# Attention in turns of two steps, with the array's small tiles kept together

## The reference

```python
x = x + 0.5 * ffn(layernorm(x))          # 256 -> 1024 -> 1024 -> 256
x = x + attention(layernorm(x))          # 16 heads of 16 dims
x = x + 0.5 * ffn(layernorm(x))          # the same weights as the first

# ffn: each weight matrix is +1 or -1, from a boolean
h = s0 * (concat([x, -x]) @ w0); h = relu(h) * 2
h = s1 * (h @ w1);               h = relu(h) * 2
h = s2 * (h @ w2)

# attention, per batch and head
scores = softmax(q @ k.T / sqrt(16))     # 2048 x 2048 per head and batch
att = scores @ v
out = att @ wo.T + bo
```

## Time and profile before

| what | value |
|---|---|
| median of 3 runs | 1521.37 us |
| the profiled execution: time, span | 1521.35 us, 1517.2 us |
| PE busy | 1509.4 us (99%), 12471 matmuls |
| ACT busy | 1129.3 us (74%) |
| DVE busy | 573.5 us (38%) |
| POOL busy | 59.6 us (4%) |
| granted TensorE clock | 1.00 of full speed |

### The profile page before, as it was taken

One profiled execution on the slowest core, in us unless ns is written; L12 is line 12 of the kernel. 1 busy time (PEld: TensorE's weight loads), 2 busy tenths in 40 slices (PEclk: granted clock), 3 DMA queues, 4 the chain that ended last, 5 costly groups with the idle time before them and its releaser, 6 DMA issues.

```text
span 1517.2 us, 31574 instructions
## 1 busy us (share of the span) xinstructions
PE 1509.4 (99%) x12471; PEld 604.4 (40%) x12471; DVE 573.5 (38%) x1298; ACT 1129.3 (74%) x1654; POOL 59.6 (4%) x65
## 2 busy tenths in 40 slices
PE   8999999999999999999999999999999999999999
PEld 4555455334333333433333333333333333333354
DVE  7645764511431253234333233241332323332462
ACT  3221222898898998899889889888888988998721
POOL 2010011001000100010100000000000000000000
PEclk9999999999999999999999999999999999999999
DMA  4122323212231331232223113112213212311110
GB/s 139 42 84 48 78 77 113 75 44 81 83 82 41 96 96 41 67 105 71 81 54 95 40 53 95 40 40 67 81 40 68 81 40 54 107 47 34 36 42 16
DMA packets 110139, 101.46 MB, mean 67 GB/s; under 512 B 55846, under 2 KB 95526, under 8 KB 109990
## 3 DMA queue, kind: packets, MB, share of 16 engines
q1 hardware_dynamic: 109158, 98.60, 22.8%
q10 hardware_dynamic: 832, 0.79, 0.2%
HBM read 61.87 MB, written 25.43 MB: 58 GB/s over the span
## 4 chain that ended last, share of the span: by engine, by line
PE 99%; DVE 0%; DMA 0%; ACT 0%; issue 0%
PE psum L890 31%; PE psum L852 30%; PE psum L874 16%; PE psum L752 12%; PE psum L764 3%; PE psum L740 3%; PE psum L771 2%; PE psum L784 1%; PE psum L777 0%; DMA x_sb<-in_x 0%; DVE stats L1032 0%; DVE xn L974 0%; PE psum L712 0%; DVE x_sb L989 0%; ACT xn L913 0%
## 5 line engine op out<-in xcount | busy, mean ns | idle before, releaser
L944 ACT ACTIVATE prob<-psum 128x512 f32<-128x512 f32 (+1 forms) x1438 | 1016.6, 784 | 120.0 <-PE psum L874 115.5
L890 PE MATMUL psum<-prob,v_sb 128*17 128x512 f32 x4096 | 489.4, 595 | 0.0
L874 PE MATMUL psum<-q_st,k_st 64*128 64x512 f16 x2048 | 350.1, 379 | 0.2
L917 ACT ACTIVATE h_hi<-psum 128x512 f16<-128x512 f32 x183 | 109.6, 604 | 211.9 <-PE psum L752 160.7
L982 DVE TENSOR_SCALAR h_hi<-psum 128x512 f16<-128x512 f32 x73 | 50.5, 692 | 434.0 <-PE psum L852 434.0
L984 DVE SCALAR_TENSOR_TENSOR h_lo<-psum,h_hi 128x512 f16<-128x512 f32 x256 | 168.7, 687 | 83.4 <-ACT h_hi L917 80.9
L890 PEld LDWEIGHTS psum<-prob,v_sb 128*17 128x17 f32 x4096 | 95.2, 96 | 263.0 <-issue 166.4
L874 PEld LDWEIGHTS psum<-q_st,k_st 64*128 64x128 f16 x2048 | 82.5, 94 | 279.1 <-ACT prob L944 210.7
L852 PE MATMUL psum<-h_hi,w 64*128 64x512 f16 x1184 | 152.1, 376 | 0.2 <-ACT h_hi L917 0.2
L852 PE MATMUL psum<-h_lo,w 64*128 64x512 f16 x1184 | 152.0, 376 | 0.0
L752 PE MATMUL psum<-h_hi,w 128*128 128x512 f16 x432 | 102.1, 379 | 0.0
(11 more groups left out here) (109 smaller groups left out, 857.1 us busy)
## 6 DMA issues: line engine op xcount, KB each, us to landing
k_st<-k_halves SPq DMA_DIRECT2D x64, 512.0 KB, 4.4
q_halves<-piece SPq DMA_DIRECT2D x32, 256.0 KB, 2.5
q_st<-q_halves SPq DMA_DIRECT2D x64, 128.0 KB, 5.0
x_rows<-x_sb SPq DMA_DIRECT2D x16, 256.0 KB, 2.2
k_halves<-piece SPq DMA_DIRECT2D x16, 256.0 KB, 2.8
att_rows<-o_sb SPq DMA_DIRECT2D x128, 32.0 KB
x_sb<-x_rows SPq DMA_DIRECT2D x8, 512.0 KB, 4.1
att_t<-att_rows SPq DMA_DIRECT2D x16, 256.0 KB
```

Source lines behind the costliest of these rows:

```text
L874: mm = pe.matmul(psum[:, score_bank[h + r], :], k_st[rows, slot, t * P:(t + 1) * P], q_st[rows, slot, :], start=True, stop=True)
L890: mm = pe.matmul(psum[32 * j:32 * j + va, O_BANK, :], v_sb[:, b * key_tiles + t, GROUP * g4 + j, :], prob[:, h % PROBS, :], start=(t == 0) ...
L917: act.activation(hi, psum[:, bank, :], ACT.Relu).then_inc(act_done, 1)
L944: act.activation(prob[:, to:to + count, :], psum[:, bank:bank + count, :], ACT.Exp, scale=score_scale / QK_SCALE ** 2).then_inc(exp_sem, 1)
```

## The change

Attention now goes in turns of two steps, after a first step that has scores and side slots alone. A turn begins with wide work: four times a group of side slots (`GAP`: 4 of l2, 8 of l3, 1 of qk, 2 of v or `out`) and a score pair behind each. Then come four tiles of products, with a narrow score pair behind each. In turns of l1 the second half of the 16 slots stands in the narrow part and is narrow too.

A product with v is split into two matmuls, one for each half of 64 keys; the lower half goes into bank 4 and the upper into bank 5 (`O_BANKS`), and `dve_o` copies one and adds the other. Narrow scores and narrow slots have each 128-column matmul cut into four of 32 columns (`columns_of`), so everything in the narrow part runs on tiles of 64 rows and 32 columns. The score ring has four banks, always used as two neighbouring pairs, and all exps take two banks. `sq` moves from the score ring to the side banks, between products.

PE's program, steady work of l2, before: the end of one step and the start of the next (L874 scores, L890 products with v).

The diff, cut:

```diff
+    narrow: bool = False
     mate: object = None
...
-    SCORES = [0, 1, 2, 3, 4]
-    O_BANK = 5
+    O_ZEROED = 1
+    SCORES = [0, 1, 2, 3]
+    O_BANKS = [4, 5]
...
         if behind == blocks:
             steps.append(Step("range", blocks - 1))
         if ahead is not None:
             steps += [Step("l1", ahead, m) for m in range(2)]
-            if after and not early:
-                steps.append(Step("sq", behind))
             steps += [Step("l1", ahead, m) for m in range(2, kh)]
...
     ahead_of_attention = [s.kind in FILLS for s in side[:[(s.kind, s.u) for s in side].index(("l2", qblocks + 1))]]
-    in_turn = SCORES[:4] + SHARED + SCORES[4:]
+    in_turn = SCORES + SHARED + O_BANKS[1:]
...
-    PAIRS = {"l1": (4, 4), "l2": (5, 3), "l3": (10, 6), "qk": (1, 1), "v": (2, 2), "out": (2, 2)}
+    GAP = {"l1": 4, "l2": 4, "l3": 8, "qk": 1, "v": 2, "out": 2}
+    o_left = numbers.held[O_BANKS[1]]
...
                 find[bank.kind, bank.u, bank.m] = bank
             s.hi = 0
         lo, s.hi = s.hi, s.hi + slots
-        work.append(replace(s, lo=lo, hi=s.hi, n=2 * s.n, mate=t))
+        work.append(replace(s, lo=lo, hi=s.hi, n=2 * s.n, mate=t, narrow=narrow))
         if s.hi == 2 * s.n:
             s.lo, s.hi = 0, s.n
...
-
-    for n in range(att_steps):
-        work.append(Step("att", n))
-        lay_scores(n)
-        work.append(Step("score", n, 0))
+    scores_left = [numbers.held[bank] for bank in SCORES]
+
+    def lay_score(no, narrow=False):
+
+        n, pair = divmod(no, STEP_BANKS // 2)
+        if pair == 0:
+            work.append(Step("att", n))
+        work.append(Step("score", n, pair, narrow=narrow))
+
+    def lay_values(tile):
+        work.append(Step("values", tile // 2, tile % 2))
+
+    def lay_turn(n):
+
         lay_idle(n)
         if side[0].kind != "l2":
             lay_long(math.inf)
-        elif n >= 4 and side[0].hi + sum(PAIRS["l2"]) < 2 * FILLS["l2"][0]:
+        else:
             lay_long(1.0)
 
-        for between, slots in enumerate(((5, 3), (3, 3), (3, 2), (3, 2))[n] if n < 4 else PAIRS[side[0].kind]):
-            lay_pair(slots)
-            work.append(Step("score", n, 1 + between))
-        if n == 0:
-            lay_pair(8)
-        if columns and not side[0].n:
-
-            lay_exps(n, ((0, 1), (1, 2), (3, 1), (4, 1), (5, 2), (7, 1)))
-            lay_column(columns.pop(0))
+    def lay_column():
+
+        if side[0].kind in ("sq", "range"):
+            lay(side.pop(0), SHARED, False)
+
+    lay_score(0)
+    lay_score(1)
+    lay_turn(0)
+    lay_pair(5)
+    lay_score(2)
+    lay_pair(5)
+    lay_score(3)
+    lay_pair(6)
+
+    for n in range(1, att_steps, 2):
+        no, tile, whole = 4 * n, 2 * (n - 1), n + 1 < att_steps
+        lay_turn(n)
+        if side[0].kind == "l1" and whole:
+            for _ in range(2):
+                lay_pair(4)
+                lay_score(no)
+                no += 1
+            for _ in range(2):
+                lay_values(tile)
+                lay_score(no, True)
+                no, tile = no + 1, tile + 1
+            lay_turn(n)
+            for _ in range(2):
+                lay_pair(4, True)
+                lay_score(no, True)
+                no += 1
+            for _ in range(2):
+                lay_values(tile)
+                lay_score(no, True)
+                no, tile = no + 1, tile + 1
         else:
-            lay_exps(n, ((0, 1), (1, 2), (3, 2), (5, 2), (7, 1)))
-        if n:
-            work.append(Step("values", n - 1))
-            if n % group_steps == 0:
-                work.append(Step("o", n // group_steps - 1))
-        if n == group_steps * (groups // 2 - 1):
+            gap = GAP[side[0].kind]
+            for _ in range(4):
+                lay_pair(gap)
+                lay_score(no)
+                no += 1
+            if side[0].kind == "l2" and side[0].n:
+                lay_long(1.0)
+            for between in range(4):
+                lay_values(tile)
+                if between == 2:
+                    lay_column()
+                if whole:
+                    lay_score(no, True)
+                no, tile = no + 1, tile + 1
+        if (n + 1) % group_steps == 0 and whole:
+            work.append(Step("o", n // group_steps))
+        if n == group_steps * (groups // 2) - 7:
 
             assert ("v", blocks - 1, 1) in find
-    work.append(Step("values", att_steps - 1))
     work.append(Step("o", groups - 1))
 
...
     while side:
-        lay(side.pop(0), TAIL, True)
+        s = side.pop(0)
+        lay(s, TAIL, True)
+        if s.kind in FILLS and s.bank == O_BANKS[1] and s.free_act == s.free_dve == 0:
+            s.free_o = O_ZEROED + groups
     done_fast = (numbers.mm, numbers.act, numbers.dve)
 
...
+                    pe_scores(s.u, s.m, s.narrow)
                 elif s.kind == "values":
-                    pe_values(s.u)
+                    pe_values(s.u, s.m)
                 elif s.kind == "att_end":
 
-                    pe.wait_ge(exp_sem, len(exp_groups))
+                    pe.wait_ge(exp_sem, exp_no(STEP_BANKS * att_steps - 1))
...
+        def columns_of(narrow):
+
+            width = P // 4 if narrow else P
+            return [slice(c, c + width) for c in range(0, P, width)]
+
...
+                        mm = pe.matmul(psum[c, bank.bank, wide], w[:, c], a,
+                                       start=(turned == 0 and j == 0), stop=(turned == 1 and j == length - 1))
                     if i == 2 * n - 1:
                         mm.then_inc(mm_done, 1)
                     elif not turned and j == length - 1:
                         mm.then_inc(halves, 1)
 
-        def pe_scores(n, pair):
+        def pe_scores(n, pair, narrow):
             g, tp = divmod(n, group_steps)
             t = 2 * tp + pair // 2
             slot = g % 2 * 2 + pair % 2
             h = STEP_BANKS * n + 2 * pair
-            for r in range(2):
...
-                    pe.wait_ge(exp_sem, exp_done[left])
-                elif kind == "dve":
-                    pe.wait_ge(dve_done, left)
-                else:
-                    pe.wait_ge(act_done, left[0])
-                    pe.wait_ge(dve_done, left[1])
+            if h < len(SCORES):
+                for act_left, dve_left in scores_left[h:h + 2]:
+                    pe.wait_ge(act_done, act_left)
+                    pe.wait_ge(dve_done, dve_left)
+            else:
+                pe.wait_ge(exp_sem, exp_no(h + 1 - len(SCORES)))
             for r in range(2):
                 rows = slice(64 * r, 64 * r + 64)
-                mm = pe.matmul(psum[:, score_bank[h + r], :], k_st[rows, slot, t * P:(t + 1) * P], q_st[rows, slot, :],
-                               start=True, stop=True)
+                for c in columns_of(narrow):
+                    mm = pe.matmul(psum[c, SCORES[(h + r) % len(SCORES)], :], k_st[rows, slot, t * P:(t + 1) * P][:, c],
+                                   q_st[rows, slot, :], start=True, stop=True)
             mm.then_inc(qk_sem, 1)
 
-        def pe_values(n):
+        def pe_values(n, tile):
             g, tp = divmod(n, group_steps)
             b, g4 = g // (qblocks * block_groups), g % block_groups
-            for tile in range(2):
-                t = 2 * tp + tile
-                if t == 0:
-                    pe.wait_ge(o_copied, O_ZEROED + g)
-                    pe.wait_ge(dve_done, find["v", (b + 1) * qblocks - 1, 1].dve)
-                for j in range(GROUP):
-                    h = STEP_BANKS * n + GROUP * tile + j
-                    if j % 2 == 0:
-                        pe.wait_ge(exp_sem, exp_done[h + 1])
-                    mm = pe.matmul(psum[32 * j:32 * j + va, O_BANK, :], v_sb[:, b * key_tiles + t, GROUP * g4 + j, :],
-                                   prob[:, h % PROBS, :], start=(t == 0), stop=(t == key_tiles - 1))
-                mm.then_inc(pv_sem, 1)
+            t = 2 * tp + tile
+            if n == 0 and tile == 0:
+                pe.wait_ge(act_done, o_left[0])
+                pe.wait_ge(dve_done, o_left[1])
+            if t == 0:
+                pe.wait_ge(o_copied, O_ZEROED + g)
+                pe.wait_ge(dve_done, find["v", (b + 1) * qblocks - 1, 1].dve)
+            for j in range(GROUP):
+                h = STEP_BANKS * n + GROUP * tile + j
+                if j % 2 == 0:
+                    pe.wait_ge(exp_sem, exp_no(h))
+                for r in range(2):
+                    rows = slice(64 * r, 64 * r + 64)
+                    mm = pe.matmul(psum[32 * j:32 * j + va, O_BANKS[r], :],
+                                   v_sb[rows, b * key_tiles + t, GROUP * g4 + j, :], prob[rows, h % PROBS, :],
+                                   start=(t == 0), stop=(t == key_tiles - 1))
+            mm.then_inc(pv_sem, 1)
 
         def pe_attention(n):
...
-                    act.wait_ge(pv_sem, (last - PROBS) // GROUP + 1)
-                bank, to = score_bank[h], h % PROBS
```

(18 more changed lines are left out.)

70 lines of the change are left out of this document (15 added, 55 removed).

## The result

The changed kernel takes 1503.33 us, the median of 4 runs (1502.64 to 1504.59); the kernel before, run beside it, 1521.45 (1521.27 to 1521.71). The ratio is 0.9882, 95% interval [0.9867, 0.9897]: 18.1 us faster. The forecast was 1508 us, its own range 1500 to 1515.

What follows compares the result with a forecast made beforehand. PE bounds attention, losing 0.23 us per step at two tile-shape changes. Merging -29.4, start spread +15.4 and narrow side slots +1 make -13 against 1521.35: 1508 us, own range 1500 to 1515, full range 1489 to 1535.

Steps and rivals of the forecast that it cites:

- What bounds the kernel: Attention: PE shows no idle time but loses 0.23 us per step at two tile-shape changes, 59 us over 256 steps.
- Gain of merging, -29.4: Attention turns: one change there and back per two steps, 128 instead of 256, at 0.23 us each, gains 29.4 us.
- Eight tiles cost more than four, +15.4: Narrow part: start spread grows where product and score orders alternate, net 0.12 us per turn, 15.4 us taken back.
- 28d: Last tile's lateness per turn, d being the start spacing between tiles: 0.14 us with d = 5 ns.
- The rows at 778: Trace of column sums and products at 778 us, read as showing tiles keep their own time and spreads never close.
- rival of full gain: Narrow part: spreads don't grow, or close at each pass; 1492 us, up to 1499 with part growth; chance 0.20.
- The estimate that I made from it, 1504: Narrow part: the skill's 4 ns tile spacing gives 28 x 4 = 0.11 us and a time near 1504.
- Narrow side slots, +1: Turns of l1: 0.2 us of cover left at the second pair; 1 us charged for 18 turns, bounds 0 to 5.
- Four banks, 0: Score ring: with score pairs 1.08 us apart, four banks and paired exps cost nothing; 0.7 us slack, 0.2 behind a relu.
- The copy of o, 0: Group ends: the added 0.7 us DVE operation costs nothing, hidden beneath 4.6 us before the next group's first product.
- Narrow tiles at full rate: Narrow part: eight 64x32 tiles stream as two 64x128 or four 128x32 tiles do, keeping array time at 8.62 us.
- the rivals that spoke against it (0.43 us, or 25 ns from start to start): Narrow fp16 tiles take 0.43 us, 1639 us, chance 0.05; 25 ns starts, some 58 us slower, 0.02 inside that.

Runs made afterwards that it cites:

- The two experiments with other counts: Changed kernel with turns of one step, 1532.67 us; changed kernel with all scores and slots wide between the products, 1596.12 us.

## Why the prediction was right, and where it was off

**What bounds the kernel: right.** PE's chain, and in it the changes of shape. The two experiments with other counts put one at 0.115 (half of 0.229) and 0.123 us.

**Gain of merging, -29.4: right, in part by chance.** -29.3, from the kernel with turns of one step. The forecast took 0.23 us for each change there and back. A turn of l2 gave 0.26 to 0.27 (the 0.23 and the larger spread of the way back), the others 0.17 to 0.20, and the mean happens to be 0.229.

**Eight tiles cost more than four, +15.4: the step that failed.** "The last tile is late by 7d + 21d = 28d" was wrong. Its spacing was nearly right, d = 6.5 ns in place of 5, and 28d would have been 0.18 us. What is there is 7d, 0.045 us, once per turn: against 0.02 before that is 0.026 us more for each way back, 3.3 us in all. The kernel with turns of one step bears the small size out: two steps of l2 take 9.12 to 9.13 us there and took 9.08 before, so 0.02 to 0.03 more for each way back, where the forecast's growth over its three crossings (7d + 9d) gives 0.06 to 0.08. The spread is set where narrow work begins and is handed on; orders that cross, seven times per turn, add nothing. A single start shows how: in a crossing, a tile started 0.197 us after its own last start, where a round comes every 0.216, so it did not wait for the full distance. The rows at 778 were read rightly as far as they went: a spread that a wait had made was handed on. They showed no growth, and the forecast added it. By the forecast's own signs the spread spoke for its rival of full gain ("the spread stays near 0.03"), and the turn of l2, 8.87 us, lies below the 8.9 to 9.0 named for it; the time of that rival, 1492, did not come because of the losses that follow.

The Trainium skill's figure of about 4 ns from one packed tile to the next (TensorE: Matmul & The Clock Gate, section Part 3) is nearer to the 3 to 8 ns here than the 25 ns of the same page (section Wait — 56ns, not 53.3ns?), which no start in a round keeps to. The estimate that I made from it, 1504, came out close for the wrong reason: it had the growth too.

**The saving is not the same in all turns: not in the sum.** I took every turn as one of l2. Lengths of two steps before and of a turn after, by what fills them:

| filling | turns | two steps before | turn after | saved |
|---|---|---|---|---|
| l2 | 63 | 9.077 | 8.867 | 0.21 |
| l3 | 18 | 9.11 | 8.96 | 0.15 |
| qk | 8 | 9.11 | 9.09 | 0.02 |
| out | 7 | 9.13 | 9.18 | -0.05 |
| v | 4 | 9.19 | 9.11 | 0.08 |
| l1, three turns | 9 x 3 | 27.61 | 27.29 | 0.32 |

If all had saved 0.21, attention would be 7.6 us shorter (1.0 + 1.5 + 1.8 + 0.5 + 2.8, from l3 down). The cause is shown for qk, v and out: their fp32 slots now stand right behind the change, where the old order had a score pair (L874 x4 in the earlier trace rows), and one wide pair there made each of these 19 turns 0.09 us shorter. The rest of their loss fits the wait for `halves` in mid-turn, which the old order did not have there (slots start 0.26 us behind the score and not 0.22, and an fp32 one takes 0.10 longer); no run takes it away. For l3 the same wait shows in the starts (0.26 for 0.22). In l1 a wait for `halves` was there before, at 0.26; in the narrow part it takes 0.32 in each of 18 turns, some 1.1 us, and the pause of 0.8 us at 1287 is in the 2.8 as well. That these are all of the loss of l1 and l3 is only argued.

**Narrow side slots, +1:** the margin of 0.2 us at the second pair of l1 held in all 18 turns (the first narrow slot starts 0.215 to 0.217 us behind the score). The loss with l1, 2.8 us, has the other causes above.

**Four banks, 0: right,** and by the reason given, the even 1.08 us. ACT's load did fall, as the forecast said ("less than now"), if the lengths of the exps are added up (1127 us before, 1049 after); its busy time, which counts overlapping exps once, rose by 25 us. It stayed off the path, at 77%.

**The copy of o, 0: right 31 times of 32.** For the last group there is no next turn to hide it. The addition, 0.7 us, and the 3.45 us of side slots that went from behind attention into it, made a wait of 2.6 us, which the kernel with `out` later took away.

**Narrow tiles at full rate: right;** the rivals that spoke against it (0.43 us, or 25 ns from start to start) fell.

So the sum, against the profile: -29.4 + 3.3 + 7.6 makes -18.5, which is what the 127 turns measure (1157.4 to 1138.9); attention's start and end bring it to -20.1; what stands behind gives back 3.3. That makes -16.8 in that execution, and -18.1 between the medians. One pause, two starts 1.09 us apart at 1287.2 to 1288.3, is in the turns: it too ends 1.6 us behind a packet of q8, as the 47 of the kernel that is narrow throughout, so the changed kernel itself ran short of instructions once. A term that was 12 us too dear stood in for losses of 11 us that the forecast had at nothing; that the result fell within 5 us is partly luck.

## What to carry to other kernels

On a full TensorE look for changes of tile shape, count them and multiply by a price read from the trace (0.12 us here), then group work of one shape as far as its buffers allow; narrow filler between narrow products lets a group be longer than buffers for wide filler would. Before you price all repeats alike, read one of each kind: what stands first behind a change or a wait (fp32 above all) costs extra, and behind a change one cheap matmul pair in front of it hid that here. Count the instructions too: narrow matmuls are four times as many. And follow the chain behind the last repeat, where nothing hides it.
